# Accumulation banks of the first graph attention: rotated over the heads

## The reference

```python
xl = (x @ W).reshape(n, heads, out_ch)
alpha_src = jnp.einsum('nhc,hc->nh', xl, a_src)
alpha_dst = jnp.einsum('nhc,hc->nh', xl, a_dst)
e = jax.nn.leaky_relu(alpha_src[src] + alpha_dst[dst], 0.2)
m = jax.ops.segment_max(e, dst, num_segments=n)
e = jnp.exp(e - m[dst])
s = jax.ops.segment_sum(e, dst, num_segments=n)
alpha = e / (s[dst] + 1e-16)
out = jax.ops.segment_sum(xl[src] * alpha[:, :, None], dst, num_segments=n)
```

## Time and profile before

| | |
|---|---|
| runs | 913.14, 913.3, 914.49 us; median 913.3 |
| profiled execution | 913.32 us; its span from first to last instruction 911.5 us |
| TensorE matmul busy | 839.1 us, 92% of the span |
| TensorE weight loads | 548.4 us, 60% |
| VectorE busy | 680.3 us, 75% |
| ScalarE busy | 308.7 us, 34% |
| mean granted clock of TensorE | 0.969 |
| L817, the first attention's products | 800 passes, 185.3 us busy, 28.3 us idle before them |

### The profile page before, as it was taken

One profiled execution on the slowest core, in us unless ns is written; L12 is line 12 of the kernel. 1 busy time (PEld: TensorE's weight loads), 2 busy tenths in 40 slices (PEclk: granted clock), 3 DMA queues, 4 the chain that ended last, 5 costly groups with the idle time before them and its releaser, 6 DMA issues.

```text
span 911.5 us, 13876 instructions
## 1 busy us (share of the span) xinstructions
PE 839.1 (92%) x5086; PEld 548.4 (60%) x5086; DVE 680.3 (75%) x1179; ACT 308.7 (34%) x531; POOL 60.4 (7%) x82
## 2 busy tenths in 40 slices
PE   3999998999699999999999877968999999999995
PEld 2677775566454444447888756856656666655553
DVE  5988885787665759778767788775985588965686
ACT  3344444400011101118777555563212108730000
POOL 2000001000102000100000000000110000000021
PEclk8899999899899999999999989989999999999998
DMA  8000002223301222522031013110222642312231
GB/s 287 1 3 2 2 2 59 99 77 145 152 37 47 78 80 87 186 81 98 22 114 29 30 52 105 58 40 1 70 70 70 216 137 70 104 70 70 70 104 66
DMA packets 23374, 70.43 MB, mean 77 GB/s; under 512 B 2628, under 2 KB 3548, under 8 KB 23182
## 3 DMA queue, kind: packets, MB, share of 16 engines
q1 hardware_dynamic: 21438, 61.80, 19.7%
q0 software_dynamic: 1872, 7.78, 2.8%
HBM read 49.26 MB, written 20.31 MB: 76 GB/s over the span
## 4 chain that ended last, share of the span: by engine, by line
PE 61%; DVE 19%; issue 11%; DMA 3%; ACT 2%; POOL 2%; DVEq 0%; SPq 0%; POOLq 0%; ACTq 0%
PE psum L636 16%; PE psum L788 13%; PE psum L817 12%; PE psum L879 11%; DVE arena L1224 6%; PE psum L665 4%; DVE arena L1325 2%; DVE arena L1329 2%; DVE arena L1348 1%; DVE arena L1192 1%; DMA arena<-as_scratch 1%; ACT arena L953 1%; PE psum L670 1%; ACT arena L965 1%; DVE arena L1356 1%
## 5 line engine op out<-in xcount | busy, mean ns | idle before, releaser
L636 PE MATMUL psum<-arena 128*128 128x512 f16 (+1 forms) x1080 | 228.2, 363 | 0.9 <-DVE arena L1219 0.9
L817 PE MATMUL psum<-arena 128*128 128x257 f32 x800 | 185.3, 394 | 28.3 <-ACT arena L953 22.2
L886 ACT ACTIVATE arena<-psum 128x160 uint16<-128x160 f32 (+6 forms) x226 | 95.1, 466 | 331.4 <-PE psum L636 79.5
L817 PEld LDWEIGHTS psum<-arena 128*128 128x128 f32 x800 | 156.7, 198 | 55.7 <-issue 21.3
L636 PEld LDWEIGHTS psum<-arena 128*128 128x128 f16 x1080 | 100.2, 98 | 103.9 <-issue 5.1
L788 PE MATMUL psum<-arena 128*128 128x512 f16 x960 | 159.2, 328 | 2.4 <-ACT arena L953 2.4
L788 PEld LDWEIGHTS psum<-arena 128*128 128x128 f16 x960 | 94.4, 98 | 64.9 <-ACT arena L953 2.8
L965 ACT ACTIVATE arena<-arena 128x640 f32<-128x640 f32 x160 | 119.1, 829 | 13.9 <-DVE arena L1329 6.6
L879 PE MATMUL psum<-arena 128*128 128x512 f16 (+2 forms) x600 | 98.4, 326 | 0.0
L1325 DVE TENSOR_TENSOR arena<-arena 128x640 f32<-128x640 f32 x80 | 65.5, 819 | 33.9 <-ACT arena L965 32.9
L1234 DVE CUSTOM_DVE_ANT_0 arena<-psum,arena 128x256 bf16<-128x256 f32 (+1 forms) x100 | 46.7, 527 | 52.6 <-PE psum L636 33.1
(11 more groups left out here) (161 smaller groups left out, 619.1 us busy)
## 6 DMA issues: line engine op xcount, KB each, us to landing
arena<-in_L_gnn_W_dram SPq DMA_DIRECT2D x14, 384.0 KB, 5.4
r_scratch<-arena SPq DMA_DIRECT2D x10, 512.0 KB, 2.6
arena<-uv_scratch SPq DMA_DIRECT2D x16, 320.0 KB, 3.7
arena<-r_scratch SPq DMA_DIRECT2D x10, 512.0 KB, 3.6
x_scratch<-arena SPq DMA_DIRECT2D x10, 384.0 KB, 4.5
arena<-x_scratch SPq DMA_DIRECT2D x10, 384.0 KB, 3.6
r_scratch<-arena SPq DMA_DIRECT2D x10, 384.0 KB, 2.6
arena<-r_scratch SPq DMA_DIRECT2D x10, 384.0 KB, 3.8
```

Of the source, the lines that this page charges most:

```text
L636: ins = pe.matmul(o[:, a:b], part[:, k, ds(t * P, P)], w[:, k, a:b], start=(not begun and k == 0 and n == 0 and m == 0), stop=(k == kn - 1 ...
L817: last = pe.matmul(p_att[:, j, 0:HID + 1], pf[n % PSLOTS][:, j * P:(j + 1) * P], xl[ch % H][:, k, 0:HID + 1], start=(k == 0), stop=(k == T ...
L886: act.activation(out_, in_, ACT.Copy, scale=scale).then_inc(signal, 1)
```

## The change

```diff
+ATT_BANKS = [[(ch * C1 + j) % 8 for j in range(C1)] for ch in range(H)]
+ATT_BANKS += [[(4 + ch * C1 + j) % 6 for j in range(C1)] for ch in range(H)]
+
+def bank_reader(ch, j):
+    users = [c * C1 + i for c in range(ch) for i in range(C1) if ATT_BANKS[c][i] == ATT_BANKS[ch][j]]
+    return users[-1] + 1 if users else 0
+
+def bank_runs(ch):
+    starts = [j for j in range(C1) if j == 0 or ATT_BANKS[ch][j] != ATT_BANKS[ch][j - 1] + 1] + [C1]
+    return list(zip(starts, starts[1:]))
...
-        p_att = psum[:, 0:512 * C1].rearrange("p (j n) -> p j n", j=C1)
+        p_att = psum.rearrange("p (b n) -> p b n", b=8)
...
-                    if k == 0 and ch:
-                        pe.wait_ge(S["att_read"], (ch - 1) * C1 + j + 1)
-                    elif k == 0 and j in (2, 4):
+                    if k == 0 and bank_reader(ch, j):
+                        pe.wait_ge(S["att_read"], bank_reader(ch, j))
+                    elif ch == 0 and k == 0 and j in (2, 4):
                         pe.wait_ge(S["r1_read"], T - 2 + j // 2)
-                    last = pe.matmul(p_att[:, j, 0:HID + 1], pf[n % PSLOTS][:, j * P:(j + 1) * P],
+                    last = pe.matmul(p_att[:, ATT_BANKS[ch][j], 0:HID + 1], pf[n % PSLOTS][:, j * P:(j + 1) * P],
...
-                    act.activation(att[ch // H * C1 + j][:, ch % H * HID:(ch % H + 1) * HID], p_att[:, j, 0:HID], ACT.Copy,
+                    act.activation(att[ch // H * C1 + j][:, ch % H * HID:(ch % H + 1) * HID], p_att[:, ATT_BANKS[ch][j], 0:HID], ACT.Copy,
...
-                dve.tensor_scalar(ssum, p_att[:, :, HID:HID + 1].rearrange("p j n -> p (j n)"), SOFTMAX_EPS, None, ALU.add).then_inc(S["dve"], 1)
-                dve.wait_ge(S["dve"], steps_done(1))
+                for a, b in bank_runs(ch):
+                    first = ATT_BANKS[ch][a]
+                    dve.tensor_scalar(ssum[:, a:b], p_att[:, first:first + b - a, HID:HID + 1].rearrange("p j n -> p (j n)"),
+                                      SOFTMAX_EPS, None, ALU.add).then_inc(S["dve"], 1)
+                dve.wait_ge(S["dve"], steps_done(len(bank_runs(ch))))
```

## The result

The changed kernel takes 910.64 us (median of 6 runs, 909.38 to 911.03); the kernel before, on the same chips, 914.72 us (6 runs, 913.14 to 918.04). The ratio is 0.9945, 95% interval [0.9929, 0.9962]: faster, by 4.1 us between the medians, where 3.95 were forecast. The profiled execution took 910.84 us, its span is 908.9 us. The ratios of this document leave out one execution, of 4854.58 us, of the run with the rotation in the second half alone.

The account below looks back on a forecast made before the run. TensorE was taken to bound the first half and tail of the first attention, VectorE with its waits the second half. Terms -3.80 + 0.28 - 0.43 = -3.95 us gave 909.4 us; 8-in-10 range 907.3 to 911.3.

Parts of the forecast that it names:

- the three terms: First attention stage: first half -3.80 us, second half +0.28, tail -0.43, together -3.95.
- The first half, -3.80: Heads 1 to 3, TensorE's path: three free groups gain 1.29 us a change of head, 1.22 at one, 3.80 in all.
- head 1's second instruction: Head 1's sums take two VectorE instructions, holding back head 2's fourth group: 0.07 us lost on the first half's path.
- the held fourth group: At changes to heads 1 to 3, the fourth group's weight load waits 0.20 us for the previous head's first eviction.
- D: Rival: TensorE loses full clock at changes to heads 1 to 3, making the kernel slower, 917.8 us; chance 0.03.
- VectorE stays ready: First half: VectorE still waits 0.5 to 0.9 us for TensorE at the sums, so TensorE stays the later.
- the cover for the fourth tile: First half: three tiles in hand last to 442.8 us, VectorE's next weights are done at 442.2; cover about 0.5 us.
- The three late gaps stay: Second half: TensorE's gaps of 6.60, 5.55 and 5.77 us stay above 5 us, since VectorE is late by itself.
- The second half, +0.28: Head 3's to head 6's sums: second sums instructions in heads 3 to 6 cost 4 x 0.07 = 0.28 us.
- moves as a block: The 98.75 us from head 3's to head 6's sums are VectorE's own and shift together, apart from the 0.28 us.
- The tail, -0.43, with the clock between -1.5 and +1.3: Head 7: one group done before the wait saves 0.43 us; the low-clock stretch could change that by -1.5 to +1.3.
- The next stage's clock, -1.7 to +1.1: Behind the stage's end, TensorE's low-clock stretch at 632.0 to 635.7 us could shift the time by -1.7 to +1.1 us.

Follow-up runs that it names:

- the four runs with the full change: Full change alone 910.64 us; with 13 unread TensorE products 909.64; with ScalarE evicting later in heads 4 to 7 901.84; with both edits 897.4.
- six banks alone: Changed kernel with rotation over six banks in all eight heads, one free group per change of head in the first half: ratio 0.9988 to the kernel before.
- idle products: Changed kernel plus 13 unread TensorE products behind the first free group in heads 5, 6 and 7: 909.64 us, ratio 0.994 to the kernel before.

## Why the prediction was right, and where it was not

The direction, its place and nearly its size were right: 909.4 against 910.64 us, -3.95 against -4.1. The mechanism of the main term is shown by the experiments. That the two numbers lie 0.15 us apart is in part luck: in the profiled pair the three terms come to -2.23, since second half and tail missed by 0.45 and 1.4 us the same way, and the rest of the 4.1 lies in executions that no trace shows.

- *The first half, -3.80.* Measured -3.93. The pitch is 21.68, 21.69 and 21.67 us where 21.70 to 21.77 was written; the 0.07 for head 1's second instruction is not seen in it. Of the 1.49 us 0.18 are left: 21.68 less 21.50. At the change to head 2 the weight loads stop for 0.16 us and go on right behind the end of the first read, as the held fourth group should:

```profile
458.43 1.93 ACT L969 ACTIVATE arena<-psum,arena 128x256 f32<-128x256 f32 x5 [5.02 <-DVE arena L1336]
458.96 5.07 PEld L833 LDWEIGHTS psum<-arena 128*128 128x128 f32 x24
```

At the changes to heads 1 and 3 no such stop is listed, so that the hold makes up all of the 0.18 there is not shown. The clock stayed up, so that D has nothing, and the Trainium skill's swing of the clock (TensorE: Matmul & The Clock Gate, A second HAM failure mode: psum-queue depth-cycling) does not appear here. The window over the change to head 2:

```profile
458.00:480.00 22.00, 22.00 (x103) 19.18 (x102) 16.48 (x25) 16.55 (x25) 0.00 (x0) 1.00 0.20 76
```

- *VectorE stays ready.* Right: it waits 0.88, 0.82 and 0.77 us for TensorE, 0.5 to 0.9 having been written; the cover for the fourth tile held.
- *The three late gaps stay.* Right in the main: 6.14, 4.62 and 5.55 us, one of them below the 5 that was written, and the experiment with the second half alone has all seven waits. This is also where the Trainium skill's rule (Perfetto Trace Analysis, Matmuls), to rotate groups through the banks, meets its limit: it gives the gain at the three changes where the eviction was late because TensorE had just finished, and nothing at the three where VectorE had not come to the sums.
- *The second half, +0.28.* Mis-sized: +0.73. The price of a second instruction was right (0.06 for 0.07; the trace has three of them inside the stretch), but the stretch was not as rigid as "moves as a block" says. 0.46 us are the VectorE wait in head 5 shown above, and the two weight transfers on the path took 3.06 and 3.16 us in the chain after, 2.97 and 3.08 before. That wait stands in the four runs with the full change, and not in those with the first half, the second half or six banks alone, nor in those with fixed banks. In these four VectorE's program is the same and the wait stands at the same instruction, 12.95 us behind head 4's sums with the clock low (after) and held (idle products) alike. In the others VectorE's program is another one. So it goes with that program; by what is open: neither the clock nor the second instruction by itself.
- *The tail, -0.43, with the clock between -1.5 and +1.3.* This step is where the profiled execution lost most: +0.97, the early group's -0.43 and a low stretch that came out 1.4 us dearer, just outside the +1.3 that was given. That the size is the clock's is shown by the idle products; that it is longer in the runs with six banks was not foreseen, and why it is stays open.
- *The next stage's clock, -1.7 to +1.1.* Wrong: it is not on the path. After the change the low stretch there is gone (1.00 where it was 0.54):

```profile
629.50:631.00 1.50, 1.49 (x9) 0.90 (x10) 0.60 (x1) 0.86 (x1) 0.00 (x0) 1.00 0.00 0
631.00:633.00 2.00, 2.00 (x14) 1.19 (x13) 1.97 (x4) 0.00 (x0) 0.00 (x0) 1.00 0.00 0
```

and yet from head 7's sums to the end of the span it is 281.8 us in both (911.5 - 629.67 and 908.9 - 627.10). I had read a low clock as a loss of time without asking whether TensorE sets the end there.

## What to carry to other kernels

A gap of an engine is worth what the engine that ends it could have done earlier. Look at whether the releasing instruction itself waited: where the sums waited for TensorE, more banks paid per free group; where the sums came late by VectorE's own work and waits, free banks paid nothing, and moving ScalarE's eviction behind the next exponentials paid about twice as much as the banks did. And a stretch of low clock counts only where its engine is on the path.

## What the runs showed of the hardware

- How long TensorE stays at its lower level behind a gap does not follow from the gap's length: 3.02 us of low clock behind a gap of 5.77 us before, 5.86 us behind one of 5.55 us after, and 4.1 us behind one of 5.77 us with rotation in the first half alone. On the path the difference between before and after is 1.4 us.
- Products that nobody reads, put into a wait on TensorE, kept the granted clock at 1.00 in the tail and shortened it by 2.2 us in one kernel and 2.85 us in another.
- A small VectorE instruction that reads PSUM right behind another of its kind, with no wait between, adds 0.06 to 0.07 us.
